# Soft-expert stages: the preparation of tokens reordered by groups of two batches

## The reference

```
xn = _layernorm(x, ln_gamma, ln_beta)
x_unit = _l2norm(xn, axis=-1)                     # x / max(sqrt(sum x^2), 1e-12)
mu_unit = _l2norm(mu, axis=0)
logits = einsum('bnd,des->bnes', x_unit * scale, mu_unit)
dispatch = softmax(logits, axis=1)                # over the tokens of a batch
combine = softmax(logits.reshape(B, N, E * S), axis=-1)
slot_in = einsum('bnd,bnes->besd', xn, dispatch)
h = gelu(einsum('besd,edh->besh', slot_in, w1) + b1)
slot_out = einsum('besh,ehd->besd', h, w2) + b2
out = einsum('besd,bnes->bnd', slot_out, combine)
```

## Time and profile before

| | us |
|---|---|
| median of three runs | 1045.39 |
| lowest, highest | 1043.42, 1049.7 |
| the profiled execution: time | 1045.39 |
| its span | 1043.6 |
| PE busy | 789.7 (76%) |
| DVE busy | 675.5 (65%) |
| ACT busy | 511.3 (49%) |
| POOL busy | 429.7 (41%) |

### The profile page before, as it was taken

How to read it: one execution, slowest core, us unless ns; L and a number is a source line. 1 busy time by engine, 2 the same in 40 slices (tenths; PEclk the granted TensorE clock), 3 DMA queues, 4 the chain that set the end, 5 groups by cost and what they waited for, 6 DMA issues and landing times.

```text
span 1043.6 us, 18846 instructions
## 1 busy us (share of the span) xinstructions
PE 789.7 (76%) x5628; PEld 520.1 (50%) x5628; DVE 675.5 (65%) x2458; ACT 511.3 (49%) x1374; POOL 429.7 (41%) x495
## 2 busy tenths in 40 slices
PE   4689882987598840798834888988989898828977
PEld 3578772646497830576711322433433333316757
DVE  4555555685755549465662787888888897564644
ACT  5323331524143315665310366757667677667660
POOL 1047772300277735110632476475475533261100
PEclk9999996895599975799965588989989899969998
DMA  5821123002011140000013442232222300000002
GB/s 148 246 62 49 49 48 89 1 18 63 18 51 50 48 99 0 1 2 1 2 20 49 55 62 32 34 57 31 42 46 31 50 4 3 3 0 1 1 1 82
DMA packets 53427, 42.97 MB, mean 41 GB/s; under 512 B 9861, under 2 KB 48722, under 8 KB 53328
## 3 DMA queue, kind: packets, MB, share of 16 engines
q1 hardware_dynamic: 45920, 30.96, 14.7%
q0 software_dynamic: 4992, 9.32, 3.4%
q10 hardware_dynamic: 2416, 1.48, 0.7%
HBM read 18.27 MB, written 11.40 MB: 28 GB/s over the span
## 4 chain that ended last, share of the span: by engine, by line
PE 44%; DVE 17%; issue 13%; ACT 10%; POOL 8%; DMA 5%; ACTq 1%; SPq 1%; DVEq 0%; POOLq 0%
PE psum L1417 6%; POOL arena L821 5%; PE psum L1402 4%; PE psum L1357 3%; ACT arena L1566 3%; PE psum L1195 3%; PE psum L738 3%; PE psum L1158 3%; PE psum L1167 2%; PE psum L1389 2%; DVE cst L1475 2%; DVE half_stats L439 2%; PE psum L776 2%; POOL result_rows L829 2%; PE psum L1256 2%
## 5 line engine op out<-in xcount | busy, mean ns | idle before, releaser
L1475 DVE CUSTOM_DVE_ANT_0 cst<-psum,rot 128x512 bf16<-128x512 f32 (+3 forms) x512 | 222.8, 486 | 69.1 <-PE psum L1389 63.8
L1566 ACT ACTIVATE arena<-psum 128x512 f32<-128x512 f32 (+1 forms) x384 | 177.9, 533 | 59.4 <-PE psum L1402 52.9
L1389 PE MATMUL psum<-arena 48*128 48x512 bf16 (+3 forms) x512 | 123.2, 334 | 38.4 <-DMA arena<-cut 22.6
L821 POOL DMA_INDIRECT arena<-xhat_rows,gather_row x78 | 76.8, 984 | 154.5 <-DVE scatter_row L638 131.3
L1402 PE MATMUL psum<-arena 51*128 51x512 bf16 (+3 forms) x512 | 113.8, 318 | 11.3 <-ACT arena L1566 7.9
L1653 POOL TENSOR_SCALAR_AFFINE_SELECT arena<-arena 128x384 f32<-128x384 f32 x128 | 63.9, 524 | 128.0 <-ACT arena L1566 127.8
L1417 PE MATMUL psum<-arena 128*32 128x512 f32 (+3 forms) x1024 | 100.3, 491 | 1.9 <-POOL arena L1656 1.9
L829 POOL DMA_INDIRECT result_rows<-arena,scatter_row x78 | 78.6, 1007 | 31.6 <-issue 21.4
L788 PE MATMUL psum<-arena 128*128 x624 | 90.8, 290 | 0.1
L776 PE MATMUL psum<-arena 128*128 128x128 f32 x624 | 87.3, 285 | 1.3 <-DVE arena L650 1.2
L788 PEld LDWEIGHTS psum<-arena 128*128 128x128 f32 x624 | 78.0, 196 | 6.3 <-issue 0.3
(11 more groups left out here) (249 smaller groups left out, 1697.9 us busy)
## 6 DMA issues: line engine op xcount, KB each, us to landing
arena<-cut SPq DMA_DIRECT2D x180, 64.0 KB
xhat_rows<-xh SPq DMA_DIRECT2D x16, 256.0 KB, 2.3
arena<-result_rows SPq DMA_DIRECT2D x8, 512.0 KB, 6.1
x<-in_L_attn_x SPq DMA_DIRECT2D x4, 512.0 KB, 7.7
arena<-in_L_ffn_w SPq DMA_DIRECT2D x1, 2048.0 KB, 9.6
out<-x SPq DMA_DIRECT2D x4, 512.0 KB, 3.2
arena<-xhat_rows,gather_row POOLq DMA_INDIRECT x78, 2.6
result_rows<-arena,scatter_row POOLq DMA_INDIRECT x78, 2.3
```

Of the source, the lines that this page charges most:

```text
L821: pool.indirect_dma_start(xg[:, j % AHEAD, :], None, xhat_dram, bass.IndirectOffsetOnAxis(gather_row[:, j:j + 1], 0)).then_inc(gathered[j ...
L1389: mm = pe.matmul(to[:, col:col + (k + 1) * P], q_stack[b % STACKS][rows, h, k * P:k * P + P], k_stack[b % STACKS][rows, h, 0:(k + 1) * P], ...
L1475: last = nc.vector.tensor_tensor_reduce(masked_scores[:, number % 2, col:col + n_keys], frm[:, col:col + n_keys], mask[:, S - n_keys:], 1. ...
L1566: nc.scalar.activation(prob_e[g % 2][:, j, first:last], bank[MAX_BANKS + number % EXP_BANKS][:, 0:last - first], ACT.Exp, scale=DH ** -0.5 ...
```

## The change

Nothing is computed differently; the order of instructions in the two mix stages is. The norms go by quarter of the tokens (one group, 8 tiles) instead of by half (16 tiles), with `norm_sqrt` and `unit_ready` counting 4 instead of 2.

- Stage 3 (`between` is true): the hook on DVE, called as groups are finished inside the ffn's last loop, now also adds beta of group g - 1 and makes the norms of group g - 2. ACT squares group 0 between its centring of groups 1 and 2, group 1 between those of groups 2 and 3.
- Stage 5 (`between` is false): the hook only centres, as before. In `vector` the additions of beta and the norms of the quarters alternate. ACT squares quarters 0, 1 and 2, copies xT and squares quarter 3.
- Both: POOL's order is gamma for groups 0, 1, 2, the unit vectors of batch 0, gamma for group 3, and then the other unit vectors.

```diff
@@ -917,7 +917,7 @@
         BY_ACT = 6
-        MIX_COUNTS = dict(v=0, centered=GROUPS * BY_ACT, centered_v=GROUPS * (GT - BY_ACT), scaled=B, xn=B, squared=T, norm_sqrt=2, unit_ready=2, unit=B, turned=T,
+        MIX_COUNTS = dict(v=0, centered=GROUPS * BY_ACT, centered_v=GROUPS * (GT - BY_ACT), scaled=B, xn=B, squared=T, norm_sqrt=GROUPS, unit_ready=GROUPS, unit=B, turned=T,
                           xT_ready=B, logit_c=2 * B, logit_d=2 * B, max_c=2 * B, max_d=2 * B, exp_c=T, exp_d=2 * B,
                           turn_c0=B, turn_c1=B, turn_d0=B, turn_d1=B, kept_c0=B, kept_c1=B, kept_d0=B, kept_d1=B,
                           in_mm=B, in_kept=2 * B, in_turned=B, slotT=B, h_mm=MG, h_gelu=MG * MG, out_mm=4, out_kept=4,
@@ -932,7 +932,30 @@
                     nc.vector.tensor_scalar(xn[:, t, :], x[:, t, :], mean[:, t:t + 1], rstd[:, t:t + 1],
                                             ALU.subtract, ALU.mult).then_inc(s["centered_v"], 1)
-            after_finish[n] = centre_vector
+            def shift_vector(g):
+                for b in (2 * g, 2 * g + 1):
+                    nc.vector.wait_ge(s["scaled"], at["scaled"] + b + 1)
+                    tiles = xn[:, TB * b:TB * b + TB, :]
+                    nc.vector.tensor_tensor(tiles, tiles, beta[:].unsqueeze(1).to_broadcast([P, TB, D]), ALU.add).then_inc(s["xn"], 1)
+
+            def unit_vector(g):
+                norm, unit = st[:, 3, :], st[:, 4, :]
+                c = slice(GT * g, GT * g + GT)
+                nc.vector.wait_ge(s["norm_sqrt"], at["norm_sqrt"] + g + 1)
+                stats_chain(nc.vector.tensor_scalar(norm[:, c], st[:, 2, c], 1e-12, None, ALU.max))
+                stats_chain(nc.vector.reciprocal(unit[:, c], norm[:, c]))
+                nc.vector.tensor_scalar(unit[:, c], unit[:, c], mscale[:, 0:1], None, ALU.mult).then_inc(s["unit_ready"], 1)
+
+            between = stages[n - 1] == "f"
+
+            def front_vector(dve, g):
+                centre_vector(dve, g)
+                if between and g >= 1:
+                    shift_vector(g - 1)
+                if between and g >= 2:
+                    unit_vector(g - 2)
+
+            after_finish[n] = front_vector
             def vector(dve):
                 chain = Chain(dve, s["v"], chains["m"])
@@ -940,18 +963,20 @@
                     slots_unit_first(dve)
                     slots_unit_last(dve, chain)
-                for b in range(B):
-                    dve.wait_ge(s["scaled"], at["scaled"] + b + 1)
-                    tiles = xn[:, TB * b:TB * b + TB, :]
-                    nc.vector.tensor_tensor(tiles, tiles, beta[:].unsqueeze(1).to_broadcast([P, TB, D]), ALU.add).then_inc(s["xn"], 1)
-
-                norm, unit = st[:, 3, :], st[:, 4, :]
-                for half in range(2):
-                    c = slice(T // 2 * half, T // 2 * half + T // 2)
-                    dve.wait_ge(s["norm_sqrt"], at["norm_sqrt"] + half + 1)
-                    chain(nc.vector.tensor_scalar(norm[:, c], st[:, 2, c], 1e-12, None, ALU.max))
-                    chain(nc.vector.reciprocal(unit[:, c], norm[:, c]))
-                    nc.vector.tensor_scalar(unit[:, c], unit[:, c], mscale[:, 0:1], None, ALU.mult).then_inc(s["unit_ready"], 1)
+                stats_chain.engine = dve
+                if between:
+                    shift_vector(GROUPS - 1)
+                    unit_vector(GROUPS - 2)
+                    unit_vector(GROUPS - 1)
+                else:
+                    shift_vector(0)
+                    shift_vector(1)
+                    unit_vector(0)
+                    shift_vector(2)
+                    unit_vector(1)
+                    shift_vector(3)
+                    unit_vector(2)
+                    unit_vector(3)
                 def max_c(b):
                     for j in range(2):
@@ -1030,17 +1055,19 @@
             def gpsimd(pool):
                 pool.wait_ge(mixw_in, MIXW)
-                for b in range(B):
-                    if b % 2 == 0:
-                        pool.wait_ge(s["centered"], at["centered"] + BY_ACT * (b // 2) + TB)
-                    else:
-                        pool.wait_ge(s["centered"], at["centered"] + BY_ACT * (b // 2 + 1))
-                        pool.wait_ge(s["centered_v"], at["centered_v"] + (GT - BY_ACT) * (b // 2 + 1))
-                    tiles = xn[:, TB * b:TB * b + TB, :]
-                    pool.tensor_tensor(tiles, tiles, gamma[:].unsqueeze(1).to_broadcast([P, TB, D]), ALU.mult).then_inc(s["scaled"], 1)
+
+                def scaled(g):
+                    for b in (2 * g, 2 * g + 1):
+                        if b % 2 == 0:
+                            pool.wait_ge(s["centered"], at["centered"] + BY_ACT * g + TB)
+                        else:
+                            pool.wait_ge(s["centered"], at["centered"] + BY_ACT * (g + 1))
+                            pool.wait_ge(s["centered_v"], at["centered_v"] + (GT - BY_ACT) * (g + 1))
+                        tiles = xn[:, TB * b:TB * b + TB, :]
+                        pool.tensor_tensor(tiles, tiles, gamma[:].unsqueeze(1).to_broadcast([P, TB, D]), ALU.mult).then_inc(s["scaled"], 1)
                 def units(b):
-                    pool.wait_ge(s["unit_ready"], at["unit_ready"] + b // (B // 2) + 1)
+                    pool.wait_ge(s["unit_ready"], at["unit_ready"] + b // 2 + 1)
                     h = b % 2
                     tiles = slice(TB * b, TB * b + TB)
                     if b >= 2:
@@ -1048,7 +1075,12 @@
                     pool.tensor_tensor(xh[:, TB * h:TB * h + TB, :], xn[:, tiles, :], st[:, 4, tiles].unsqueeze(2).to_broadcast([P, TB, D]),
                                        ALU.mult).then_inc(s["unit"], 1)
-                for b in range(B):
+                scaled(0)
+                scaled(1)
+                scaled(2)
+                units(0)
+                scaled(3)
+                for b in range(1, B):
                     units(b)
                 pool.memset(hid_diag[:], 0.0).then_inc(s["cleared"], 1)
@@ -1059,16 +1091,16 @@
                         nc.scalar.activation(xn[:, t, :], x[:, t, :], ACT.Identity, bias=shift_by[:, t:t + 1],
                                              scale=rstd[:, t:t + 1]).then_inc(s["centered"], 1)
-                def squares(half):
-
-                    for t in range(T // 2 * half, T // 2 * half + T // 2):
+                def squares(g):
+
+                    for t in range(GT * g, GT * g + GT):
                         if t % TB == 0:
                             act.wait_ge(s["xn"], at["xn"] + t // TB + 1)
                         if t >= GT:
                             act.wait_ge(s["squared"], at["squared"] + t - GT + 1)
                         nc.scalar.activation(square[:, t % GT, :], xn[:, t, :], ACT.Square, accum_out=st[:, 5, t:t + 1]).then_inc(s["squared"], 1)
-                    act.wait_ge(s["squared"], at["squared"] + T // 2 * half + T // 2)
-                    c = slice(T // 2 * half, T // 2 * half + T // 2)
+                    act.wait_ge(s["squared"], at["squared"] + GT * g + GT)
+                    c = slice(GT * g, GT * g + GT)
                     nc.scalar.activation(st[:, 2, c], st[:, 5, c], ACT.Sqrt).then_inc(s["norm_sqrt"], 1)
                 def copy_xT(b, h):
@@ -1110,15 +1142,23 @@
                     exp_d(b + 1, 1 - h)
                 stats_root(act, n, 0)
-                for g in range(1, GROUPS):
-                    stats_root(act, n, g)
-                    centre(g - 1)
-                centre(GROUPS - 1)
-                if early < 0 and n == stages.index("m"):
-                    slots_unit_scalar(act)
-                squares(0)
+                stats_root(act, n, 1)
+                centre(0)
+                stats_root(act, n, 2)
+                centre(1)
+                if between:
+                    squares(0)
+                stats_root(act, n, 3)
+                centre(2)
+                if between:
+                    squares(1)
+                centre(3)
+                if not between:
+                    squares(0)
+                    squares(1)
+                squares(2)
                 copy_xT(0, 0)
-                squares(1)
+                squares(3)
                 exp_c(0, 0)
                 exp_d(0, 0)
                 step(0, 0)
```

## The result

The changed kernel took 1035.41 us (median of 4 runs, 1034.98 to 1036.24), the kernel before 1046.03 in the same comparison: ratio 0.9895, 95% interval 0.9867 to 0.9922, or 10.6 us (8.2 to 13.9 by the interval). The profiled execution took 1035.48 us with a span of 1033.7, 9.9 us less than before.

The account below looks back on a forecast made before the run. TensorE was taken to stand idle (42.7 us behind the ffn) until the soft-expert preparation delivers the first xT copy and exponential. Terms 3.1 + 3.0 + 1.7 = 7.8 us off 1045.39 gave 1037.6 us; range 1034.5 to 1045.5.

Parts of the forecast that it names:

- L688's last eight at 403.1 us, done before POOL's pair is: Ffn's tail: the last eight results start 1.2 us later, take 2.18 us, and end 2.34 us before POOL's second gamma pair.
- Two turns lost in the first norm chain, group 3 six us late: Stage 3: DVE's norms of quarter 0 lose two turns to POOL; group 3 is ready at 414.7 instead of 408.6 us.
- ACT sets the exponential: Stage 3: after group 3 is ready, ACT's own work leads to the first exponential at 424.35 instead of 428.40 us.
- Term 1: Stage 3, behind the ffn: batch 1's logits start earlier, 3.1 us won, between 1.7 and 4.0.
- Term 2: Stage 5, behind attention: first exponential at 940.15 instead of 943.16 us, 3.0 us won, between 1.2 and 3.6.
- a reciprocal that never waits: Rival, norm chains: DVE's reciprocal loses no turn to POOL; 0.6 us more won in stage 5, 1037.0 us; chance 0.12.
- Term 3: Stage 5: a shorter TensorE pause keeps its clock up, batch 1's logits 1.99 instead of 3.68 us; 1.7 us, between 0 and 1.7.
- TensorE's pace from the earlier xT alone: Rival, both stages: TensorE stays longer at half clock, only the earlier xT copies count, 1.7 and 1.2 us; 1042.5 us; chance 0.18.
- turns lost in the tail: Rival, ffn's tail: DVE loses eight more turns to POOL, overrunning the 4.0 us margin at stage 3's exponential; 1051 us; chance 0.05.

Follow-up runs that it names:

- e6: Changed kernel with beta of group 0 in stage 3 moved from before the ffn's last eight results to behind them; 1034.8 us, ratio 0.9902 to the kernel before.
- e7: Changed kernel with DVE's scale and centring of group 3 in stage 3 ahead of beta 1 and group 0's norms; 1034.91 us, ratio 0.9900 to the kernel before.
- e2: Changed kernel with stage 3 back in the old order but norms by quarter, stage 5 as changed; 1038.64 us, ratio 0.9953 to the kernel before.
- e4: Kernel before with 16 unused transposes put into TensorE's pause in stage 5; 1043.06 us against 1043.52, ratio 0.9999.
- c3: The kernel before, unedited, run once more; 1045.16 us, ratio 0.9995.
- e1: Changed kernel with stage 5 back in the old order but norms by quarter, stage 3 as changed; 1040.16 us, ratio 0.9972 to the kernel before.
- e8: As e6, but ACT centres four tiles of a group instead of six, in both stages; 1035.45 us, ratio 0.9910 to the kernel before.
- e5: Changed kernel with POOL's gamma of group 1 in stage 3 waiting for the ffn's last results; 1031.93 us, ratio 0.9906 to the kernel before.
- c2: As e6, and in stage 5 beta of group 2 ahead of group 0's norms; 1032.07 us, ratio 0.9875 to the kernel before.

## Why the prediction was right

1037.6 us was forecast and 1035.41 measured; 7.8 us of gain against 10.6. The range held it, 0.9 us from its lower end; it lies 0.1 us outside the 1035.5 to 1040 that had most of the chance. The gain is 1.05%, on the 1% bound, and 0.08 was too small a chance for more than that: the sum of its own upper bounds was 9.3 us, and the gain of D was in no bound.

- *L688's last eight at 403.1 us, done before POOL's pair is.* Wrong: a tie, and POOL went first. 2.0 us lost on L688, group 3's root 25.00 us behind the first results instead of the 23.5 that the forecast gives (408.56 - 385.07). e6, where DVE starts earlier, has 23.50.
- *Two turns lost in the first norm chain, group 3 six us late.* Half right: one long wait in the chain (0.88) and one in group 3's shift (1.08), group 3's centring at 415.71. (The sum there is 0.2 us short: 410.6 + 0.64 + 2 x 1.2 is 413.6, not 413.4; nothing hangs on it.) Called the price of the change, it was none: ACT squared quarter 1 until then, as the same part said, and e7 shows that an earlier group 3 gives nothing.
- *ACT sets the exponential.* Right. Forecast 39.28 us behind the first results, measured 39.58 (on the scale from 385.07 and 385.50). That it is so close is in part luck: group 3's root came 1.5 us late, but the forecast also had ACT stand still for 0.8 us before group 3's centring (413.9 to 414.7), and that wait was not there.
- *Term 1, 3.1 us.* Mechanism right, size off: 3.75. I let TensorE's logits and next transposes keep their 7.14 us; they took 5.66 (421.22 to 426.28 + 0.60), since its clock came up some 3.0 us sooner after the first logit: PEclk is 0.84 for 424 to 425 us now and was 0.89 for 428 to 429 before, 0.50 up to there in both, with the first logits at 421.22 and 422.13. At half clock 3.0 us do the work of 1.5. So the exponentials' gain counted whole, near the upper bound of 4.0.
- *Term 2, 3.0 us.* 3.3, in e2 as well. The rival of a reciprocal that never waits was true as a mechanism: 0.20 us in each of the three chains where it met POOL at work (412.73, 418.76 and 929.75). Its 0.6 us came half true; that the other 0.3 went into the product behind it, which still waits a turn, is argued and not shown. The Trainium skill, page "SBUF — State Buffer", section "Who interferes with whom", exempts single-input operations outside the two-port modes; the trace agrees for the reciprocal with its 0.20 us. Its neighbours L945 and L947 (1.23 and 0.95 us) also have one tensor as input, but they are TENSOR_SCALAR, which the same section lists among the operations that can enter those modes. So is L447, whose 1.19 us the prediction took as agreement with the rule for two inputs; the operation that shows that rule is the one before it, L446, a TENSOR_TENSOR, at 919.22 us: 1.24 us for 0.16.
- *Term 3, 1.7 us.* 1.7, and e4 obtains it from the pause alone, within stretch B.
- *What no term had:* 0.9 us in D, where the half clock fell less on work, and 0.65 in C, which lies within C's scatter. D's part is no scatter: it is 90.4 to 90.5 us in the three profiles whose batch 1 logits in stage 5 take 3.68 us (before, c3, e1; the second product takes 5.97 to 6.00) and 89.6 to 89.7 in ten of the eleven where they take 1.99 (5.10 to 5.14), e4 among them, which is the kernel before with its pause filled. So the pause of stage 5 seems to cost 0.9 us more than term 3 had. How it acts so far behind is open, and e8 does not fit (logits 1.99 us, D 90.8, second product 6.22).
- *Rivals.* TensorE's pace from the earlier xT alone (1042.5) was not seen, though e5, e6 and c2 show it as the next bound. That turns lost in the tail would make the kernel slower: turns were lost, 2.0 us of them on L688, which cost 1.3 us before the exponential and 0.6 of A (e5), well inside the margin of 4.0.

## What to carry to other kernels

When a chain of stages over all tiles sits between two matmul phases, ordering it by group brings the first result forward without taking work from anyone; most of stage 3's gain (3.4 of 3.75 us) came from that, and hardly any from starting it in the stage before. Judge the delay of a step by whether the engine that needs it has other work: six microseconds of lateness cost nothing here, with 0.65 us to spare, while a tie between DVE and POOL cost 1.3 before the exponential and 0.6 at the end of the stretch. After such a change look for what the shorter pause gives back in TensorE's clock, and read gains of a few microseconds from stretches between fixed instructions, not from the total time.

## What the runs showed of the hardware

- Where DVE and POOL held each other up, the one that started first went on through its run as long as its next operation needed no wait: POOL's pair (2.73 us) held eight DVE operations to 4.20 us, and with DVE 1.2 us earlier the same pair took 4.52 and the results 2.18. Small dependent DVE operations (128x8) that met POOL at work took 0.66 to 1.26 us instead of about 0.2, but not every one did.
- A DVE reciprocal of 128x8 took 0.20 us beside a running POOL operation (changed kernel, 412.73, 418.76 and 929.75 us).
- After a pause of 2.48 to 2.59 us before the transposes of the exponentials, TensorE's clock was still 1.00 through these transposes and fell to 0.50 behind them (before: 1.00 for 946 to 947 us, 0.52 for 947 to 948), which cost the next logits 1.69 us (3.68 against 1.99). After pauses of up to 1.70 us in that place they took 1.99 in every profile (stage 3: 1.11 us before, 1.38 in e2, 1.42 in c3, 1.70 in e4).
